# q and k of a batch multiplied a step earlier, v in the second pass, ScalarE's queue for the row maxima, and the maxima turned by transposition

## The reference

```python
# time-delay layer: 5 neighbouring frames -> 256 channels, 252 frames remain
h = relu(einsum('btk,ok->bto', windows(x, 5), W) + b)
h = gamma * (h - running_mean) * rsqrt(running_var + 1e-5) + beta
# causal attention, 16 heads of 16, with a bias by bucket of relative position
xn = layernorm(h)
sim = (xn @ Wq)(xn @ Wk)^T * 0.25 + bias, masked above the diagonal
h = h + softmax(sim) @ (xn @ Wv) @ Wo + bo
# gated feed-forward part 256 -> 768 -> 256, its weights rounded to 4 bits in blocks of 32,
# its activations to 16 bits by one largest value over the whole tensor
h = h + ffn(layernorm(h))
```

## Time and profile before

| | |
|---|---|
| median of three runs | 780.82 us (780.04 to 781.90) |
| profiled execution, its own time | 780.43 us |
| its span, first to last instruction | 778.7 us |
| busy: PE, DVE, ACT, POOL | 635.6, 599.9, 452.4, 161.6 us |
| mean granted TensorE clock | 0.921 |
| mean DMA rate | 68 GB/s |

### The profile page before, as it was taken

How to read it: one execution, slowest core, us unless ns; L and a number is a source line. 1 busy time by engine, 2 the same in 40 slices (tenths; PEclk the granted TensorE clock), 3 DMA queues, 4 the chain that set the end, 5 groups by cost and what they waited for, 6 DMA issues and landing times. The chain is left out here.

```text
span 778.7 us, 14957 instructions
## 1 busy us (share of the span) xinstructions
PE 635.6 (82%) x5257; PEld 466.1 (60%) x5257; DVE 599.9 (77%) x967; ACT 452.4 (58%) x652; POOL 161.6 (21%) x221
## 2 busy tenths in 40 slices
PE   4579999999999999999999885897999840035998
PEld 2457877777787777778777663343544310015997
DVE  7436977887888789778978887687579998896442
ACT  1436456645664665466456644435489984965762
POOL 4220223022202211231123000000022221760000
PEclk8689999999999999999999987799999985557999
DMA  6334134404430442144133410200034252600533
GB/s 192 114 47 50 20 44 63 62 13 50 61 44 18 61 61 33 28 61 61 23 41 55 57 55 13 82 1 1 0 145 175 119 197 81 214 0 0 157 123 96
DMA packets 39206, 52.83 MB, mean 68 GB/s; under 512 B 5724, under 2 KB 31772, under 8 KB 39164
## 3 DMA queue, kind: packets, MB, share of 16 engines
q1 hardware_dynamic: 38012, 51.49, 29.7%
q10 hardware_dynamic: 1152, 0.79, 0.4%
HBM read 22.74 MB, written 16.81 MB: 51 GB/s over the span
## 5 line engine op out<-in xcount | busy, mean ns | idle before, releaser
L809 DVE TENSOR_REDUCE mx<-ps 126x2 f32<-126x504 f32 (+1 forms) x192 | 125.2, 675 | 39.5 <-PE ps L653 38.8
L800 DVE TENSOR_TENSOR sbr<-ps,biasT 126x504 f32<-126x504 f32 x192 | 124.0, 676 | 24.2 <-PE ps L675 20.1
L885 ACT ACTIVATE pt<-sbr 126x504 f32<-126x504 f32 x192 | 114.4, 616 | 24.5 <-DVE sbr L800 18.7
L650 PE MATMUL ps<-biasN,antib 126*126 126x504 bf16 x192 | 75.8, 395 | 11.8 <-DMA k_st<-kl 11.8
L653 PE MATMUL ps<-k_st,q_st 65*126 65x252 f16 (+1 forms) x512 | 74.0, 246 | 0.0
L1161 PE MATMUL ps<-x2t,wgT 128*128 128x504 f16 x288 | 65.7, 388 | 9.4 <-ACT gat L1527 6.1
L675 PE MATMUL ps<-q_st,k_st 66*126 66x252 f16 (+1 forms) x512 | 68.9, 253 | 3.1 <-DMA q_st<-mneg 1.5
L653 PEld LDWEIGHTS ps<-k_st,q_st 65*126 65x126 f16 x512 | 60.1, 137 | 16.7 <-issue 1.8
L1494 PE MATMUL ps<-wdT,raws 128*126 128x256 f16 x480 | 65.5, 280 | 2.8 <-DVE raws L1438 2.8
L1161 PE MATMUL ps<-x2t,wuT 128*128 128x504 f16 x288 | 63.0, 376 | 5.1 <-ACT raws L1541 5.1
L596 PE MATMUL ps<-wcT,xh 128*126 128x256 f16 x320 | 62.3, 277 | 0.7
(11 more groups left out here) (199 smaller groups left out, 1419.3 us busy)
## 6 DMA issues: line engine op xcount, KB each, us to landing
up_raw<-raws SPq DMA_DIRECT2D x11, 756.0 KB, 3.2
x2t<-up_raw SPq DMA_DIRECT2D x6, 756.0 KB, 6.5
q_st<-qh SPq DMA_DIRECT2D x32, 128.0 KB, 3.7
k_st<-kh SPq DMA_DIRECT2D x32, 128.0 KB, 5.1
res<-hall SPq DMA_DIRECT2D x16, 252.0 KB
x2t<-res SPq DMA_DIRECT2D x16, 252.0 KB
out<-x2t SPq DMA_DIRECT2D x16, 252.0 KB
raws<-up_raw SPq DMA_DIRECT2D x5, 756.0 KB, 4.3
```

Of the source, the lines that this page charges most:

```text
L650: nc.tensor.matmul(dst, antib[0:TT], biasN[0:TT, heads[0]:heads[-1] + 1, N - w:N], start=True, stop=True)
L800: nc.vector.tensor_tensor(sbr[0:TT, n % 4].rearrange("p (h w) -> p h w", w=w), ps[0:TT, score_bank[name, n], 0:2 * N].rearrange("p (h w) - ...
L809: nc.vector.tensor_reduce(mx[0:TT, 0 if w == TT else 1, heads[0]:heads[-1] + 1], ps[0:TT, score_bank[name, n], 0:2 * N].rearrange("p (h w) ...
L885: nc.scalar.activation(pt[0:TT, n // 3 % 2, n % 3], sbr[0:TT, n % 4], ACT.Exp).then_inc(S["exp_r"], 1)
```

## The change

It has four parts.

1. q and k of a batch are multiplied at the end of the step two ahead of its P2 (offset 2 instead of 1), q between the last blocks of P1 and k in front of wo; v moves from in between the passes to the beginning of P2. The lists of the other engines follow: kl goes to the beginning of VectorE's next step, behind P2[0].
2. Other pieces move too: xT, xnT and OT come earlier against P1, xl stands ahead of stats, and xn2 earlier against the exponentials.
3. The two DMAs of mneg a batch are issued by ScalarE, right behind the instruction that makes mneg, and no longer by SP. SP now sends the stacks at the end of its step.
4. mTA and mTB are `transpose` instead of `matmul` with the identity.

```diff
-        PE_ORDER = [P2[0], P2[1], ("mTB", 0, 0), P2[2], P2[3], ("q", 1, 0), ("q", 1, 1), ("k", 1, 0), ("k", 1, 1),
-                    P2[4], P2[5], ("conv", 2, 0), P2[6], ("conv", 2, 1), P2[7], ("conv", 2, 2), ("PV", 0, 0),
-                    P2[8], ("conv", 2, 3), P2[9], ("conv", 2, 4), P2[10], ("PV", 0, 1), ("conv", 2, 5),
-                    P2[11], ("v", 1, 0), P1[0], ("v", 1, 1), P1[1], P1[2],
-                    ("PV", 0, 2), P1[3], ("xT", 3, 0), P1[4], ("PV", 0, 3), P1[5], ("x2T", -1, 0), P1[6],
-                    ("OT0", 0, 0), ("OT1", 0, 0), P1[7], ("mTA", 1, 0), P1[8], ("onT", 0, 0), P1[9], P1[10],
-                    ("xnT", 2, 0), P1[11], ("wo", 0, 0), ("wo", 0, 1)]
+        PE_ORDER = [P2[0], P2[1], ("mTB", 0, 0), P2[2], P2[3], ("v", 1, 0), P2[4], ("v", 1, 1), P2[5],
+                    ("conv", 2, 0), P2[6], ("conv", 2, 1), P2[7], ("conv", 2, 2), ("PV", 0, 0), P2[8],
+                    ("conv", 2, 3), P2[9], ("conv", 2, 4), P2[10], ("PV", 0, 1), ("conv", 2, 5), P2[11],
+                    P1[0], P1[1], ("xT", 3, 0), P1[2], ("PV", 0, 2), P1[3], P1[4], ("PV", 0, 3), P1[5],
+                    ("x2T", -1, 0), P1[6], ("OT0", 0, 0), ("OT1", 0, 0), P1[7], ("xnT", 2, 0), P1[8],
+                    ("mTA", 1, 0), ("onT", 0, 0), P1[9], ("q", 2, 0), P1[10], ("q", 2, 1), P1[11], ("k", 2, 0),
+                    ("k", 2, 1), ("wo", 0, 0), ("wo", 0, 1)]
-        DVE_ORDER = [P2[0], ("h2", -1), P2[1], P2[2], ("stats2", -1), ("ql", 1), P2[3], ("kl", 1), P2[4], P2[5]
-                     ] + P2[6:12] + P1[0:3] + [("stats", 2), P1[3], ("ax", -2), P1[4], ("xl", 3), P1[5],
-                     ("on", 0, 0), P1[6], ("on", 0, 1), P1[7], P1[8], P1[9], ("onl", 0), P1[10], P1[11], ("xnl", 2)]
+        DVE_ORDER = [P2[0], ("kl", 1), P2[1], ("h2", -1), P2[2], ("stats2", -1)] + P2[3:12] + [
+                     P1[0], P1[1], ("xl", 3), P1[2], ("stats", 2), P1[3], P1[4], ("ax", -2), P1[5], P1[6],
+                     ("on", 0, 0), P1[7], ("on", 0, 1), ("xnl", 2), P1[8], P1[9], ("onl", 0), P1[10], ("ql", 2), P1[11]]
-        ACT_ORDER = [("mnegB", 0), P2[0], P2[1], ("qh", 1), P2[2], ("kh", 1), P2[3], P2[4], P2[5], P2[6],
-                     ("osb", 0, 0), P2[7], P2[8], ("xn2", -1), P2[9], P2[10], ("relu", 2), P2[11],
-                     ("osb", 0, 1), ("va", 1), ("osb", 0, 2), ("xh", 3), ("osb", 0, 3), ("x2", -1), ("xn", 2),
-                     ("mnegA", 1), ("onh", 0), ("xnh", 2)]
+        ACT_ORDER = [("mnegB", 0), P2[0], P2[1], P2[2], ("va", 1), P2[3], P2[4], P2[5], P2[6], ("osb", 0, 0),
+                     ("xn2", -1), P2[7], P2[8], P2[9], P2[10], ("relu", 2), P2[11], ("osb", 0, 1), ("xh", 3),
+                     ("osb", 0, 2), ("osb", 0, 3), ("x2", -1), ("xn", 2), ("xnh", 2), ("mnegA", 1), ("onh", 0),
+                     ("qh", 2), ("kh", 2)]
...
-        MISC = [[("mTB", "mneg_r", 2, 2, 0), ("q", "ql_r", 1, 1, 1), ("conv", "relu_r", 1, 1, 2),
-                 ("xnT", "xnl_r", 1, 1, 2)],
-                [("k", "kl_r", 1, 1, 1), ("v", "va_r", 1, 1, 1), ("xT", "xl_r", 1, 1, 3), ("x2T", "x2_r", 1, 1, -1),
-                 ("mTA", "mneg_r", 2, 1, 1), ("onT", "onl_r", 1, 1, 0)]]
+        MISC = [[("mTB", "mneg_r", 2, 2, 0), ("conv", "relu_r", 1, 1, 2), ("xnT", "xnl_r", 1, 1, 2),
+                 ("q", "ql_r", 1, 1, 2)],
+                [("v", "va_r", 1, 1, 1), ("xT", "xl_r", 1, 1, 3), ("x2T", "x2_r", 1, 1, -1), ("mTA", "mneg_r", 2, 1, 1),
+                 ("onT", "onl_r", 1, 1, 0), ("k", "kl_r", 1, 1, 2)]]
...
-                        last = nc.tensor.matmul(bank[0:H // 2, t * TT:(t + 1) * TT],
-                                                mx[0:TT, t, half * H // 2:(half + 1) * H // 2], identf[0:TT, 0:TT],
-                                                start=True, stop=True)
+                        last = nc.tensor.transpose(bank[0:H // 2, t * TT:(t + 1) * TT],
+                                                   mx[0:TT, t, half * H // 2:(half + 1) * H // 2],
+                                                   identf[0:TT, 0:TT])
...
+                    wait(act, "mneg_r", 2 * c + half + 1)
+                    act.dma_start(qS[odd if off else par][P1_ROWS:P2_ROWS, half * H // 2:(half + 1) * H // 2],
+                                  mneg[:, half]).then_inc(S["mneg_in"], 16)
...
-                wait(sp, "mneg_in", sent)
-                wait(sp, "mneg_r", ready)
-                sp.dma_start(qS[par][P1_ROWS:P2_ROWS, H // 2:H], mneg[:, 1]).then_inc(S["mneg_in"], 16)
...
-                wait(sp, "mneg_in", sent)
-                wait(sp, "mneg_r", ready)
-                sp.dma_start(qS[odd][P1_ROWS:P2_ROWS, 0:H // 2], mneg[:, 0]).then_inc(S["mneg_in"], 16)
+            if runs(b, 2):
+                c = b + 2
...
```

More of the change, by code:

```diff
@@ L993, in sp_step @@
             odd = 1 - par
-            if runs(b, 0):
-                unregistered(sp, b)
-                sent, ready = valued(sp, 32 * b + 16), valued(sp, 2 * b + 2)
-                wait(sp, "mneg_in", sent)
-                wait(sp, "mneg_r", ready)
-                sp.dma_start(qS[par][P1_ROWS:P2_ROWS, H // 2:H], mneg[:, 1]).then_inc(S["mneg_in"], 16)
             if isinstance(b, int) and b == B - 1:
@@ L1003, in sp_step @@
                 sp.dma_start(ff_view(0), ff_dram[0]).then_inc(S["ff_in0"], 16)
[L1004 to L1017, removed]
             if runs(b, 3):
@@ L1028, in sp_step @@
                                  hall[0:TT, bass.ds(c, 1), :].rearrange("p a n -> p (a n)")).then_inc(S["spilled"], 16)
-            if runs(b, 1):
-                unregistered(sp, b)
-                sent, ready = valued(sp, 32 * (b + 1)), valued(sp, 2 * b + 3)
-                wait(sp, "mneg_in", sent)
-                wait(sp, "mneg_r", ready)
-                sp.dma_start(qS[odd][P1_ROWS:P2_ROWS, 0:H // 2], mneg[:, 0]).then_inc(S["mneg_in"], 16)
+            if runs(b, 2):
+                c = b + 2
+                if isinstance(c, int) and c == 0:
+                    wait(sp, "pool_init", 2)
+                    wait(sp, "dve_init", INIT)
+                for nm, dst, parts in (("q", qS[par], ((qh, (0, 2)), (ql, (1,)))),
+                                       ("k", kS[par], ((kh, (0, 1)), (kl, (2,))))):
+                    done = valued(sp, 12 * (c - 1))
+                    for (src, rows), ready in zip(parts, ("h_r", "l_r")):
+                        wait(sp, nm + ready, c + 1)
+                        if ready == "h_r":
+                            wait(sp, "p2_ps", done)
+                        for i in rows:
+                            sp.dma_start(dst[16 * i:16 * i + DH], src[:]).then_inc(S["stack_in"], 16)
         INIT = 2 + 2 + 4 + 1 + 1 + 2
```

## The result

| | before | changed |
|---|---|---|
| median of four runs each (before: the three above and one more) | 780.43 us (778.43 to 781.90) | 815.84 us (810.94 to 819.98) |
| ratio, 95% interval | | 1.045 [1.039, 1.051] |
| profiled execution, its own time; span | 780.43; 778.7 us | 812.64; 810.9 us |
| first mark of a step, last mark | 66.40, 459.73 us | 72.26, 493.50 us |
| from the last mark to the end | 319.0 us | 317.4 us |

The change makes the kernel 4.5% slower, where 0.4% faster was forecast. The marks (sendings of the second half of the maxima, "B" from here on) say where: 5.9 us come before the first one, 27.9 between first and last, and 1.6 are given back behind. So most of it lies in the steps.

The account below looks back on a forecast made before the run. No engine bounds by share alone; a chain through all engines sets the step. -3.8 + 2.6 + 1.5 + 1.0 - 4.2 - 0.2 = -3.1 us from 780.43, median 777.6; own range 774 to 779.3, 8 in 10 766 to 789.

Parts of the forecast that it names:

- When the second half lands: Second half of the maxima, issued at 1.4 us, lands at 3.1 to 6.5, wanted at 4.15; taken near quiet, no cost.
- round robin by packets: DMA engines alternate between queues, so the maxima wait at most one kh packet, are just in time; sum unchanged.
- the maxima land late: Rival: maxima come 1.5 us late behind kh, P2[6] and its chain move 0.8 a step, +9 us: 786; chance 0.1.
- the clock falls: Rival: TensorE's clock halves between P1[7] and onT every third step, about 1.7 us each; six falls 787, eleven 796; chance 0.2.
- Steps 1 to 5: Walk of one loop step across the engines, from P2[0] to the next: 26.2 us instead of 26.54.
- Transposition at nothing: Turning the maxima by transposition saves TensorE 0.22 us twice a step, but ends before waits, so costed at nothing.
- ScalarE sends at nothing: 32 issues of 0.7 us move from SP to ScalarE, where they have room; cost nothing.
- Ends of the loop: Terms for the loop's first and last steps: +2.6, +1.5, +1.0 and -4.2 us.
- (a): Before the first marked step: the first q and k move ahead of it, 2.62 us that come off at the other end.
- (b): Step before the first P2: bias copies ahead of relu, xl before statistics; bounds 0 to 3.4 us, taken as 1.5.
- (c): Second to last overlapped step: 26.2 us instead of 25.23, +1.0.
- (d): Last overlapped step, without convolution, q and k: about 21 us set by VectorE's blocks, against 25.18, -4.2.

Follow-up runs that it names:

- a_kbehind: Changed kernel, but SP sends the k stack (two kh, kl) only when the second half of the maxima has landed; 780.56 us, ratio 0.999.
- a_khalf: Changed kernel, but SP sends only the first kh at once, the second kh and kl when the maxima have landed; 781.36 us, ratio 1.002.
- a_klbehind: Changed kernel, but SP sends both kh at once and holds kl alone until the maxima have landed; 799.54 us, ratio 1.023.
- a_mm: Changed kernel with the maxima turned by matmul with the identity again; 813.20 us, ratio 1.040 against the kernel before.
- b_tr: Kernel before with only the maxima turned by transpose instead of matmul; 778.25 us, ratio 0.997.
- a_sp: Changed kernel, but SP sends the maxima again; 840.15 us, ratio 1.072 against the kernel before.
- b_act: Kernel before with only the sending of the maxima moved from SP to ScalarE; 783.93 us, ratio 1.0027.

## Why the prediction was wrong, point by point

**The step that failed is "When the second half lands".** It took the quiet landing of 1.75 us "plus up to one microsecond, so no cost, because it is 4 KB against 128 KB". The landing was 5.07, B was there at 6.3 us of the step, inside the bounds of 3.1 and 6.5 that the prediction had written down itself, and close to the upper one. The size of a transfer was no reason for its landing time: a_kbehind, a_khalf and a_klbehind show it ending with the last transfer sent ahead of it. The nearest row was the 5.1 us of kh, not the quiet one, since kh was what would be under way. At the upper bound the wait is 6.5 - 4.15 = 2.35 us a step, and the sign of the forecast turns. Nor does the prediction mention ql and the second qh, sent at the end of the step before and still under way. The round robin by packets, which it set beside its choice, told when the packets are moved and not when the semaphore is full.

**The rival "the maxima land late" was the right mechanism, mis-sized twice.** It put the lateness at 1.5 (measured 1.95 to 2.3) and let only 0.8 of it through. P2[7] may start at 5.39 for VectorE's sake, and P2[6] stands 0.81 ahead of it; so everything beyond 4.6 goes through, which is 1.8 of 1.95. Even of its own 1.5 this lets 1.07 through and not 0.8. Its chance of 0.1 hung on the same choice. It also stopped at the wait: 14 x 1.86 is 26 us, and the falls added 9.

**The rival "the clock falls" was right on the price and mostly wrong on the place.** 1.7 us a fall forecast, 1.52 measured, six falls; but five come behind the wait for B, in P2, conv and PV, and only one behind the gap at onT, and in a_kbehind, which has that gap, there are none. Why that one gap lost its clock stays open. The two rivals were treated as exclusive, and they came together: without the wait for B no fall is left.

**Steps 1 to 5 were right.** With the landing mended (a_kbehind) the step is 26.17 against 26.2, P2[7] starts at 5.28 (255.27 to 260.55) against 5.39, relu at 11.0 against 11.1, onT at 20.45 against 20.5, and all three forecast waits stand at their places.

**Transposition at nothing: right** within the noise (a_mm), and b_tr shows it worth 2.6 us elsewhere. **ScalarE sends at nothing:** better than SP in this order (a_sp is slower by 2.7% of the kernel before, some 21 us), 2 us off in the old one (b_act); what the issue itself costs here was not measured.

**Ends of the loop.** (a) and (b) together were 2.6 + 1.5 = 4.1 us, measured 5.9 at the first mark. The prologue has these waits:

```profile
59.52 0.43 PE L650 MATMUL ps<-biasN,antib 126*126 126x504 bf16 x1 [1.12 <-DVE mx L809]
62.12 0.43 PE L650 MATMUL ps<-biasN,antib 126*126 126x504 bf16 x1 [1.10 <-DVE mx L809]
65.26 0.65 PE L609 MATMUL ps<-identf,xn 126*128 126x126 f32 x4 [1.66 <-ACT xn L919]
```

If (a) cost its 2.6, the 1.5 of (b) was too low by 1.8, inside its bound of 3.4. (c) was forecast as +1.0; in a_kbehind that step takes 25.81 against 25.23, so +0.6. (d) The last overlapped step: about 21 forecast, 21.43 measured with a wait for B in it, 20.65 in a_kbehind. With (b) mended the sum is -1.3 us, inside the interval of a_kbehind (-3.0 to +1.8). In a_kbehind the first mark is 8.1 us later than before and the last one stands at 459.73 as before: the gain in the steps is spent in the prologue.

## What to carry to other kernels

When a change lets two transfers meet that were apart, ask when the large ones sent ahead of a small one land: here the small one landed no sooner, even on another queue. Price it by their rows, and hold the large ones back if the small one is wanted first: here one wait on the sending engine was worth 35 us. If a rival's price rests on a bound that you wrote down yourself, work out the sum at that bound before you settle its chance. And ask what a new stall of TensorE does to its clock: rivals add up.

## What the runs showed of the hardware

- A DMA of 4 KB issued by ScalarE landed 1.76 us after its sending with nothing else under way (b_act). With stack transfers of 128 KB from SP's queue sent ahead of it, it landed after 2.15, 3.27 and 4.37 us (a_kbehind, a_khalf, a_klbehind), each time 0.03 to 0.05 us behind the last of them, and after 5.07, 0.43 behind, where one more was sent 0.6 us later (changed).
- In the changed kernel its packets had ended 2.1 us before its semaphore was full, and 1.2 us before the last packet of the transfer that it landed behind; in quiet its packets end 0.4 us before.
- Stalls of TensorE of about 2 us, followed by P2, conv and PV work, brought the clock to 1.2 GHz in five of fourteen steps; those of 1.25 us in the fourteen full steps of a_klbehind in none. Gaps of 1.0 us in front of onT brought it down in one step of the changed kernel, and in none of a_kbehind.
- Two fp32 transpositions of 126 columns were recorded with 0.38 us instead of the 0.60 of the two matmuls with the identity that they replace.
